# A graph layer on one core: edges deduplicated and scattered by chunks of 128 instead of pairs of 256

## The reference, cut to what matters

```python
xn = layernorm(x)                                   # 2500 nodes x 1024
support = xn @ W
messages = support[src] * edge_weight[:, None]      # 42500 edges
gnn = segment_sum(messages, dst, num_segments=2500)
x = x + gnn + mix(xn)                               # mix: kernelised attention of 16 heads
return x + ffn(layernorm(x))                        # ternary weights, 8-bit activations
```

## Time and profile before

| | us |
|---|---|
| median of three runs | 1879.35 |
| the profiled execution, as timed | 1875.68 |
| its span, first to last instruction | 1873.9 |
| busy: PE / DVE / ACT / POOL | 1739.3 / 1101.7 / 652.7 / 578.4 |
| POOL's scatters, first start to last start | 362.1 to 1073.9 |
| first loads of A issued by SP | 1130.9 |
| first product of stage 5 on PE | 1146.2 |

### The profile page before, as it was taken

The page is one execution under the profiler, slowest core; times in us unless marked ns, Lnnn a source line. Parts: engine busy times, 40 slices in busy tenths (PEclk is TensorE's granted clock), DMA queues, the critical chain, the costliest instruction groups (busy, mean ns, idle before and its releaser), DMA issues.

```text
span 1873.9 us, 25902 instructions
## 1 busy us (share of the span) xinstructions
PE 1739.3 (93%) x8020; PEld 1390.9 (74%) x8020; DVE 1101.7 (59%) x2583; ACT 652.7 (35%) x937; POOL 578.4 (31%) x392
## 2 busy tenths in 40 slices
PE   2379999999999899999799999899999999999797
PEld 2368788888888688888677777677777777777465
DVE  5476777877777622222456664448566584755765
ACT  1243333443333533333322221223333343333443
POOL 1011111277787787877766700000000000000000
PEclk9689999999999899999999999899999999999899
DMA  8989999976666745545787756524545344453355
GB/s 204 324 353 379 384 382 380 380 189 164 160 161 165 233 99 131 124 107 132 182 247 212 201 176 178 163 90 140 131 131 139 91 142 131 131 142 99 113 165 160
DMA packets 176137, 356.75 MB, mean 190 GB/s; under 512 B 63979, under 2 KB 112139, under 8 KB 176091
## 3 DMA queue, kind: packets, MB, share of 16 engines
q1 hardware_dynamic: 109591, 278.48, 46.1%
q0 software_dynamic: 59264, 52.62, 13.0%
q10 hardware_dynamic: 7236, 25.12, 4.6%
HBM read 238.62 MB, written 117.53 MB: 190 GB/s over the span
## 4 chain that ended last, share of the span: by engine, by line
PE 82%; DMA 6%; DVE 5%; SPq 3%; ACT 2%; issue 1%; POOL 0%; ACTq 0%; DVEq 0%; POOLq 0%
PE PS L333 25%; PE PS L335 25%; PE PS L334 24%; PE PS L1493 4%; PE PS L1518 2%; DMA uT<-usb 2%; PE PS L1382 2%; DMA xnT<-XT 1%; PE PS L1277 1%; SPq L77 1%; SPq L417 1%; DMA ewrow<-weight_rows 1%; DMA Aside<-A_dense 1%; DVE junk L345 1%; ACT hqT L904 1%
## 5 line engine op out<-in xcount | busy, mean ns | idle before, releaser
L698 POOL DMA_INDIRECT A_dense<-wtot,cell x336 | 541.9, 1613 | 183.2 <-issue 100.7
L333 PE MATMUL PS<-SL,AH 125*125 125x512 f32 x800 | 317.6, 397 | 12.0 <-DVE AL L1133 11.9
L335 PE MATMUL PS<-SH,AH 125*125 125x512 f32 x800 | 318.0, 397 | 0.0
L334 PE MATMUL PS<-SH,AL 125*125 125x512 f32 x800 | 316.2, 395 | 0.0
L333 PE MATMUL PS<-WL,xtH 128*125 128x512 f32 x640 | 257.0, 402 | 4.8 <-DVE WL L1068 2.7
L333 PE MATMUL PS<-xgL,WH 128*128 (+1 forms) x640 | 250.7, 392 | 4.7 <-issue 4.7
L335 PE MATMUL PS<-WH,xtH 128*125 128x512 f32 x640 | 253.6, 396 | 0.0
L334 PE MATMUL PS<-WH,xtL 128*125 128x512 f32 x640 | 252.8, 395 | 0.0
L334 PE MATMUL PS<-xgH,WL 128*128 (+1 forms) x640 | 250.0, 391 | 0.0
L335 PE MATMUL PS<-xgH,WH 128*128 (+1 forms) x640 | 249.6, 390 | 0.0
L1130 DVE TENSOR_TENSOR SL<-S,SH 125x1024 fp32r<-125x1024 f32 x100 | 122.3, 1223 | 169.9 <-ACT SH L843 169.9
(11 more groups left out here) (149 smaller groups left out, 2224.8 us busy)
## 6 DMA issues: line engine op xcount, KB each, us to landing
A_dense<-zeros POOLq DMA_DIRECT2D x40, 1280.0 KB, 11.0
Araw<-A_dense SPq DMA_DIRECT2D x100, 250.0 KB, 2.7
Aside<-A_dense SPq DMA_DIRECT2D x100, 250.0 KB, 2.9
xg<-xnT SPq DMA_DIRECT2D x11, 2000.0 KB, 14.1
uu<-uT SPq DMA_DIRECT2D x44, 500.0 KB, 4.5
keyrow<-key_rows SPq DMA_DIRECT2D x42, 512.0 KB, 4.9
ewrow<-weight_rows SPq DMA_DIRECT2D x42, 512.0 KB, 6.9
xt<-xnT SPq DMA_DIRECT2D x42, 500.0 KB, 5.1
```

The lines of the kernel that those rows point to most:

```text
L333: nc.tensor.matmul(o, lh, rl, start=start, stop=False)
L334: nc.tensor.matmul(o, ll, rh, start=False, stop=False)
L335: return nc.tensor.matmul(o, lh, rh, start=False, stop=stop)
L698: pool.indirect_dma_start(cells[m], bass.IndirectOffsetOnAxis(cell[:, col:col + 1], 0), wtot[:, col:col + 1], None, compute_op=ALU.add).th ...
```

## The change

Each chunk is compared with itself alone, so all four instructions of a pair have 128 columns. A scatter is a chunk: chunk c goes to matrix c % 2, and before it POOL waits until the chunk before the last, the former one on the same matrix, has landed. So up to two scatters are under way. The semaphores, SP's wait and the size of `junk` follow.

```diff
-    junk = e1("junk", [P, 2, 7, P], BF16)
+    junk = e1("junk", [P, 2, 4, P], BF16)
...
-    s_sc = [sems(f"s_sc{m}", 2) for m in range(2)]
+    s_sc = sems("s_sc", 2)
...
         for c in range(2):
             col = bass.ds(pair * 2 + c, 1)
-            nc.vector.scalar_tensor_tensor(junk[:, slot, 2 * c:2 * c + 2, :].rearrange("p a n -> p (a n)"), row,
-                                           key[:, col], wrow, ALU.is_equal, ALU.mult, accum_out=wtot[:, col])
-        nc.vector.scalar_tensor_tensor(junk[:, slot, 4, :], row[:, 0:P], key[:, bass.ds(pair * 2, 1)],
-                                       earlier[:, 1, :], ALU.is_equal, ALU.mult,
-                                       accum_out=dup[:, bass.ds(pair * 2, 1)])
-        nc.vector.scalar_tensor_tensor(junk[:, slot, 5:7, :].rearrange("p a n -> p (a n)"), row,
-                                       key[:, bass.ds(pair * 2 + 1, 1)],
-                                       earlier[:, :, :].rearrange("p a n -> p (a n)"), ALU.is_equal, ALU.mult,
-                                       accum_out=dup[:, bass.ds(pair * 2 + 1, 1)]).then_inc(s_pair[slot], 1)
+            own = slice(c * P, (c + 1) * P)
+            nc.vector.scalar_tensor_tensor(junk[:, slot, c, :], row[:, own], key[:, col], wrow[:, own], ALU.is_equal,
+                                           ALU.mult, accum_out=wtot[:, col])
+            last = nc.vector.scalar_tensor_tensor(junk[:, slot, 2 + c, :], row[:, own], key[:, col], earlier[:, 1, :],
+                                                  ALU.is_equal, ALU.mult, accum_out=dup[:, col])
+        last.then_inc(s_pair[slot], 1)
...
-            for m in range(2):
-                sp.wait_ge(s_sc[m][i], 16 * CHUNKS // 4)
+            sp.wait_ge(s_sc[i], 16 * CHUNKS // 2)
...
-        for pair in range(CHUNKS // 2):
-            m, turn = pair % 2, pair // 2
-            if pair % PAIRS == 0:
-                pool.wait_ge(s_flags, pair // PAIRS * 2 + 2)
+        for c in range(CHUNKS):
+            m, turn = c % 2, c // 2
+            if c % CH_BLOCK == 0:
+                pool.wait_ge(s_flags, c // CH_BLOCK * 2 + 2)
             if turn:
-                for c in range(2):
-                    pool.wait_ge(s_sc[m][c], turn * 16)
-            for c in range(2):
-                col = 2 * pair + c
-                pool.indirect_dma_start(cells[m], bass.IndirectOffsetOnAxis(cell[:, col:col + 1], 0),
-                                        wtot[:, col:col + 1], None, compute_op=ALU.add).then_inc(s_sc[m][c], 16)
+                pool.wait_ge(s_sc[m], turn * 16)
+            pool.indirect_dma_start(cells[m], bass.IndirectOffsetOnAxis(cell[:, c:c + 1], 0),
+                                    wtot[:, c:c + 1], None, compute_op=ALU.add).then_inc(s_sc[m], 16)
```

## The result

The changed kernel takes 1945.24 us (median of four runs, 1942.27 to 1947.64) against 1879.24 us for the kernel before (median of four, 1879.09 to 1879.56): 1.035 times as long, with a 95% interval of 1.0332 to 1.0368. That is 66 us more, where 94 were forecast. The profiled execution has a span of 1942.5 us, 68.6 more than before.

A forecast was written before the change was run, and what follows sets the result against it. PE (busy 93%) was taken to bound the kernel; the scatter would delay PE's stage 5 by 93.6 us, DVE's 2.4 gain included, plus 1 for the clock: 1879.35 + 94 = 1973 us, range 1915 to 2010.

The forecast's parts named there:

- DVE's part: Edge instructions at 128 columns: 67 us less DVE time, nearly all under full PE; 2.4 us gained at stage 2's start.
- The landing as a matter of other traffic: POOL's scatters: landings are long where other DMAs are dense, means 4.56, 4.06 and 5.37 us, and that traffic stays.
- the scatters done by 1130.9: POOL's scatters when SP stands ready for A: 286 done, 50 left at 1.95 us each, 97 us more.
- where it has to wait, it starts 0.8 us after the landing: POOL's chain: a held-back scatter starts 0.8 us after the landing it waits for.
- Half of landing plus start-up: Time per scatter on POOL with two under way: (landing + 0.8)/2, giving 2.68, 2.43 and 3.09 us by stretch.
- the floor rival: POOL's scatters: with two under way landings fall to about 3 us, scatters end in time, 1877 us; chance 0.07.
- Behind the wait: Start of stage 5: PE's first product comes 12.3 us after the first load of A, in place of 15.3.
- the clock: PE's granted clock, low for some us after the stop before stage 5: 1 us added.

The follow-up runs named there:

- e2: The changed kernel with four matrices in turn, so four scatters under way (added two neither zeroed nor read): 1876.44 us, 0.9987 of the kernel before.
- e1: The kernel before with its 256-column comparisons kept and the changed kernel's scatter (one chunk a matrix, two under way): 1948.65 us, 1.0378 of the kernel before.
- e3: The changed kernel, but each scatter waits for the one just before, so one is under way: 2441.32 us (one run).
- e6: The changed kernel with loads and stores not needing A put ahead of SP's wait, and DVE's tile 19 ahead of A's first pieces: 1943.56 us, 1.0336 of before.
- e7: The changed kernel with a second, long fulfilled wait (on the zero strips) ahead of each held-back scatter: 1984.09 us, 1.0549 of the kernel before.

## Why the prediction was right, and where its sizes were off

The direction and the mechanism held step by step: the scatter became the bound, SP's wait carried its lateness to PE, and nothing hid it. The time, 1945, lies in the range (1915 to 2010), but the delay was 66 us and not 94.

- **DVE's part** held. Its time fell by 65 us (67 forecast). Its worth, forecast at 2.4 us, agrees with e2 (0.13%, or 2.4 us), but that interval goes from 0.2 to 4.5 us, and the 3.4 us between e1 and the changed kernel lie within the noise of the two. The scatters of the changed kernel began 4.4 us earlier, not 2.4; over all profiles they begin at 356.8 to 361.3 us with narrow comparisons and at 362.1 to 366.3 with wide ones, so one pair can't tell 4.4 from 2.4.
- **The landing as a matter of other traffic** held: e3, e6 and the quiet tail show it. The Trainium skill ("DMA: Bandwidth & Descriptors", "Anatomy of one DMA — SWDGE (gpsimd) path") gives a DMA of this queue a nearly constant cost of about 2.0 us beyond its data. In the quiet tail the landings are indeed constant, but 2.9 to 3.1 us less the 1.54 on POOL leave only about 1.5. Under load, with landings of up to 9.0 us in the same kernel, the rule does not hold.
- **The term that was mis-sized** is the scatters done by 1130.9, with the rate of those left: 286 and 50 at 1.95 us forecast, 300 and 36 at 1.87 measured. Fourteen scatters fewer left at 1.9 us are 27 us, and the loads of A were 26.2 us earlier than forecast (1201.3 against 1227.5). The step behind it was "where it has to wait, it starts 0.8 us after the landing". I read that from a kernel that waits on two semaphores and used it for one that waits on one (0.27). e7 bears it out: with that second wait given back, 95, 110 and 75 scatters are done by stretch (forecast 97, 114 and 75), and the time is 1984.
- **A second error hid part of the first.** Half of landing plus start-up is too low for the time of a scatter, since a quick landing cannot be used before POOL has issued the next scatter, 1.85 us on. With 0.33 for the start-up (0.27, and 0.75 at one chunk in eight) the changed kernel's own landings give (4.48 + 0.33)/2 = 2.40, 2.13 and 2.56 us, where 2.60, 2.40 and 2.84 were measured. In the first two stretches the errors nearly cancel (2.68 and 2.43 forecast), which is luck. In stage 4 they don't (3.09), because the landing there also came out at 4.78 us and not at 5.37. Fewer under way did a part of that at most, since e6 and e7 have 5.07 and 5.04 at the same depth. At most so much of the floor rival was true.
- **Behind the wait** all was as worked out: 12.25 us from the first load of A to the first product (12.3 forecast). All the rest together is 1.3 us, where 1 was forecast for the clock; it was not taken apart.

## What to carry to other kernels

A chain of small transfers that is off the critical path has a margin, and the number of them under way is what keeps it: count how late a landing the depth covers, and compare it with the mean and the tail of the landings under load, not with the median. A start-up time read behind one kind of wait need not hold behind another. Work that fills a waiting time is free only if it does not use what the waited-for work needs.

## What the runs showed of the hardware that was not expected

A second, long fulfilled wait ahead of POOL's indirect DMA raises the time from landing to start from 0.27 to 0.75 us, and it cost 39 us over 336 scatters (e7). The landing of a 128-element scatter hardly depends on how many others are under way (4.1, 3.9, 4.0 and 4.0 us on average in stage 3 at one to four; 4.8 to 5.1 in stage 4 at one and two, 5.2 to 5.5 at three and four), and goes from 3.0 us in quiet to 11.8 at worst beside bulk loads (e6).
